# Routing the rows of a mixture of experts in five smaller batches instead of four, in one fused transformer kernel

## What is computed

```python
x = x + L0_xattn(layernorm(x), ctx, ctx)       # 16 heads, a temperature per head from a small network
x = x + L0_ffn(layernorm(x))
x = x + L1_xattn(layernorm(x), ctx, ctx)       # 8 heads, dilated windows
x = x + L1_ffn(layernorm(x))                   # 8 small experts
...
def L0_ffn(x, norm_scale, w_router, w_up, w_down):
    xn = rms_norm(x, norm_scale)
    scores_topk, idx = top_k(xn @ w_router.T, 2)          # 2 of 8 experts for each row
    weights = softmax(scores_topk)
    u, gate = split(moe_linear(each row twice, idx, w_up))  # row i times the weights of expert idx[i]
    down = moe_linear(u * silu(gate), idx, w_down)
    return sum(down * weights) + x
```

## Time and profile before

| | us |
|---|---|
| runs, median of 3 | 415.34 (414.65 to 415.39) |
| profiled execution, its own time | 413.28 |
| span of the profiled execution | 411.5 |
| busy in the span: PE | 353.8 |
| busy in the span: DVE | 303.3 |
| busy in the span: ACT | 271.8 |
| busy in the span: POOL | 196.9 |
| POOL, 32 scatters (line 942) | 32.2 |

### The profile page before, as it was taken

The page is one execution under the profiler, slowest core; times in us unless marked ns, Lnnn a source line. Parts: engine busy times, 40 slices in busy tenths (PEclk is TensorE's granted clock), DMA queues, the critical chain, the costliest instruction groups (busy, mean ns, idle before and its releaser), DMA issues.

```text
span 411.5 us, 11910 instructions
## 1 busy us (share of the span) xinstructions
PE 353.8 (86%) x4049; PEld 269.5 (65%) x4049; DVE 303.3 (74%) x1127; ACT 271.8 (66%) x813; POOL 196.9 (48%) x295
## 2 busy tenths in 40 slices
PE   2988897682599999973999999888999999968997
PEld 0524362341276767752999998757888888756886
DVE  5399989988428999996764444378898888885852
ACT  2499998986265657542578886457878778672440
POOL 4785878811002215667783000478878783532200
PEclk9988789986589999995799999989999999996999
DMA  7975739700000000112343332111001010000011
GB/s 234 338 212 160 223 100 335 322 1 0 3 2 6 6 5 18 37 34 70 105 116 92 97 92 57 37 33 41 27 23 28 17 28 2 2 2 2 4 49 51
DMA packets 36202, 30.97 MB, mean 75 GB/s; under 512 B 3504, under 2 KB 33584, under 8 KB 35504
## 3 DMA queue, kind: packets, MB, share of 16 engines
q1 hardware_dynamic: 33520, 24.98, 19.2%
q0 software_dynamic: 2048, 4.20, 3.5%
q10 hardware_dynamic: 576, 1.05, 0.7%
HBM read 14.94 MB, written 15.14 MB: 73 GB/s over the span
## 4 chain that ended last, share of the span: by engine, by line
PE 56%; DVE 19%; ACT 9%; issue 8%; POOL 4%; DMA 4%; POOLq 0%; DVEq 0%; SPq 0%; ACTq 0%
PE psum L1753 9%; ACT wa L649 6%; PE psum L1705 5%; PE psum L1545 4%; PE psum L1781 4%; PE psum L1764 4%; DVE scored L1089 3%; DVE scored L1076 3%; PE psum L1585 3%; PE psum L1894 3%; PE psum L1804 2%; PE psum L1688 2%; PE psum L1857 2%; DVE work L1131 2%; PE psum L1820 2%
## 5 line engine op out<-in xcount | busy, mean ns | idle before, releaser
L649 ACT ACTIVATE wa<-psum,scored 128x120 f32<-128x120 f32 x256 | 69.5, 436 | 3.8 <-DVE scored L1076 3.8
L983 POOL DMA_INDIRECT c_area<-by_expert,rows_at x32 | 31.4, 980 | 51.3 <-DMA by_expert<-c_area 39.7
L1089 DVE BATCH_NORM_STATS2 scored<-wa 128x6 f32<-128x240 f32 x128 | 43.1, 398 | 1.6 <-issue 0.8
L1076 DVE TENSOR_REDUCE scored<-psum 128x8 f32<-128x960 f32 x32 | 36.5, 1142 | 9.9 <-PE psum L1585 9.9
L682 ACT ACTIVATE work<-psum 120x1024 f32<-120x1024 f32 x32 | 31.0, 1021 | 18.8 <-PE psum L1693 18.8
L1753 PE MATMUL psum<-c_area,work 128*128 128x128 f32 x312 | 43.3, 284 | 0.0
L1585 PE MATMUL psum<-wa,qT 64*128 64x480 f32 x128 | 41.0, 725 | 2.3 <-ACT wa L649 2.3
L1753 PEld LDWEIGHTS psum<-c_area,work 128*128 128x128 f32 x312 | 39.7, 200 | 0.1
L910 POOL TENSOR_TENSOR rstd<-rstd,eps 128x2 f32<-128x2 f32 x16 | 12.5, 784 | 55.0 <-DVE rstd L1165 55.0
L866 POOL TENSOR_TENSOR wa<-kT,first 128x960 f32<-128x960 f32 x16 | 28.6, 1791 | 16.6 <-PE psum L1585 16.6
L942 POOL DMA_INDIRECT by_expert<-scored,rows_at x32 | 32.2, 1006 | 8.9 <-issue 8.3
(11 more groups left out here) (264 smaller groups left out, 945.0 us busy)
## 6 DMA issues: line engine op xcount, KB each, us to landing
by_expert<-work SPq DMA_DIRECT2D x12, 768.0 KB, 7.6
c_area<-by_expert SPq DMA_DIRECT2D x39, 64.0 KB, 1.8
by_expert<-c_area SPq DMA_DIRECT2D x39, 64.0 KB, 1.6
upT<-in_up_dram SPq DMA_DIRECT2D x1, 2048.0 KB, 13.7
work<-in_heads_dram SPq DMA_DIRECT2D x1, 1536.0 KB, 8.9
late<-in_late_dram SPq DMA_DIRECT2D x1, 1098.0 KB, 10.3
x<-in_x_dram ACTq DMA_DIRECT2D x4, 256.0 KB, 5.6
ctxS<-in_ctx_classes_dram SPq DMA_DIRECT2D x1, 1024.0 KB, 10.0
```

The lines of the kernel that those rows point to most:

```text
L649: e = nc.scalar.activation(prob[:, z, head, :], psum[:, score_bank(b, half) + h // 4, (h % 4) * LK:(h % 4 + 1) * LK], ACT.Exp, bias=rowneg ...
L983: nc.gpsimd.indirect_dma_start(y_rows[:, r, j, :], None, by_expert[:, :], bass.IndirectOffsetOnAxis(rows_at[:, i:i + 1], 0)).then_inc(ld_y ...
L1076: nc.vector.tensor_reduce(rowneg[:, b * H0:(b + 1) * H0].rearrange("p (a c h) -> p a c h", a=2, c=2)[:, :, half], banks(score_bank(b, half ...
L1089: s = nc.vector.bn_stats(bnout[:, bass.ds(b * HALF0 + h // 2, 1), :].rearrange("p a s -> p (a s)"), prob[:, z, h:h + 2, :].rearrange("p h ...
```

## The change

There are now five batches of 4, 3, 3, 3 and 3 sequences, so 8, 6, 6, 6 and 6 slots, and four phases of 7, 6, 6 and 20 tiles, after batches 1, 2, 3 and 4. The picks come in steps 9, 12, 15, 18 and 21 (before 9, 13, 17 and 21). The first table is two steps earlier. Scatters are two or three a step in steps 11 to 18, and the last twelve follow behind the steps. The pieces of the second table come in tiles 0 to 2, two a tile at first, those of the third in tiles 3 to 7 and of the fourth in tiles 8 to 12. In `pick_experts`, `place_rows` and `rank` the fixed numbers of sequences and slots give way to those of the batch. The core of the diff:

```diff
-BATCH = 4
-BATCHES, SLOTS = NB // BATCH, 2 * BATCH
+BATCH_SEQS = (4, 3, 3, 3, 3)
+BATCHES = len(BATCH_SEQS)
+BATCH_AT = tuple(sum(BATCH_SEQS[:r]) for r in range(BATCHES + 1))
+MOST_SLOTS = 2 * max(BATCH_SEQS)
...
+def slots_of(r):
+    return slice(2 * BATCH_AT[r], 2 * BATCH_AT[r + 1])
...
-        seqs = BATCH * (batch + 1)
+        seqs = BATCH_AT[batch + 1]
...
+def seq_at(i):
+    r = batch_of(i // 2)
+    return BATCH_AT[r] + (i - 2 * BATCH_AT[r]) % BATCH_SEQS[r]
...
-                            sp.wait_ge(scattered[r], 16 * SLOTS)
+                            sp.wait_ge(scattered[r], 16 * 2 * BATCH_SEQS[r])
...
-        PICK_AT = {BATCH * (r + 1) - 1 + LOGITS_B: r for r in range(BATCHES)}
-        TABLE_PIECES = 5
+        PICK_AT = {BATCH_AT[r + 1] - 1 + LOGITS_B: r for r in range(BATCHES)}
...
-        PIECES_AT = {15: ((0, 0),), 16: ((0, 1), (0, 2)), 17: ((0, 3),), 18: ((0, 4),)}
-        SCATTERS = {BATCH + LOGITS_B + 1 + i: range(2 * i, 2 * i + 2) for i in range((BATCHES - 1) * BATCH)}
+        PIECES_AT = {13: ((0, 0),), 14: ((0, 1), (0, 2)), 15: ((0, 3),), 16: ((0, 4),)}
+        SCATTERS_AT = ((11, 2), (12, 3), (13, 2), (14, 3), (15, 2), (16, 2), (17, 3), (18, 3))
+        SCATTERS, LOOPED = {}, 0
+        for step, count in SCATTERS_AT:
+            SCATTERS[step] = range(LOOPED, LOOPED + count)
+            LOOPED += count
+        TABLES_AT = {0: ((1, 0), (1, 1)), 1: ((1, 2), (1, 3)), 2: ((1, 4),), **{3 + i: ((2, i),) for i in range(5)},
+                     **{8 + i: ((3, i),) for i in range(5)}}
...
-                r = i // SLOTS
-                if i % SLOTS == 0:
+                r = batch_of(i // 2)
+                if i == 2 * BATCH_AT[r]:
                     pool.wait_ge(k_rows, r + 1)
                     pool.wait_ge(zeroed, 16 * (NB - 4))
...
-            for i in range(SLOTS * (BATCHES - 1), SLOTS * BATCHES):
+            for i in range(LOOPED, 2 * NB):
                 scatter(i)
...
-                if n in range(2 * TABLE_PIECES):
-                    tile_table(1 + n // TABLE_PIECES, n % TABLE_PIECES)
-                elif n == TILES - 4:
+                for piece in TABLES_AT.get(n, ()):
+                    tile_table(*piece)
+                if n == TILES - 4:
                     expert_weights()
```

More of the change, by code:

```diff
@@ L43, with batch_of, seqs_of @@
 GROUPS = NB // SEQS
-BATCH = 4
-BATCHES, SLOTS = NB // BATCH, 2 * BATCH
+BATCH_SEQS = (4, 3, 3, 3, 3)
+BATCHES = len(BATCH_SEQS)
+BATCH_AT = tuple(sum(BATCH_SEQS[:r]) for r in range(BATCHES + 1))
+MOST_SLOTS = 2 * max(BATCH_SEQS)
+def batch_of(b):
+    return next(r for r in range(BATCHES) if b < BATCH_AT[r + 1])
+def seqs_of(r):
+    return slice(BATCH_AT[r], BATCH_AT[r + 1])
+def slots_of(r):
+    return slice(2 * BATCH_AT[r], 2 * BATCH_AT[r + 1])
 class Phase:
     def __init__(self, batch, first_tile):
-        seqs = BATCH * (batch + 1)
+        seqs = BATCH_AT[batch + 1]
         self.batch, self.last, self.first_tile = batch, seqs == NB, first_tile
@@ L84, in slot_of @@
 def slot_of(j, b):
-    r, i = divmod(b, BATCH)
-    return SLOTS * r + BATCH * j + i
+    r = batch_of(b)
+    return 2 * BATCH_AT[r] + BATCH_SEQS[r] * j + b - BATCH_AT[r]
+def seq_at(i):
+    r = batch_of(i // 2)
+    return BATCH_AT[r] + (i - 2 * BATCH_AT[r]) % BATCH_SEQS[r]
 def residue(c):
@@ L165, in packs @@
                  ("expert_rows", expert_rows.reshape(P, -1))])
-    ranks = Pack([("tri", np.triu(np.ones((P, P)), 1)), ("region_rows", np.tile(np.arange(NE) * REGION, (P, SLOTS))),
+    ranks = Pack([("tri", np.triu(np.ones((P, P)), 1)), ("region_rows", np.tile(np.arange(NE) * REGION, (P, MOST_SLOTS))),
                   ("tile_no", np.tile(np.arange(MOST_TILES), (P, 1))),
@@ L338, in build @@
         tri_b, ones_b = halves(0), halves(1)
-        region_b = halves(2, SLOTS * NE)[0:1]
+        region_b = halves(2, MOST_SLOTS * NE)[0:1]
         seen = halves(3, BATCHES * NE).rearrange("p (r e) -> p r e", e=NE)
@@ L382, in build @@
         logits1 = keep[:, 256:384].rearrange("p (b e) -> p b e", b=NB)
-        rank_ps = keep[:, 512 - SLOTS * NE:512]
+        rank_ps = keep[:, 512 - MOST_SLOTS * NE:512]
         total_ps = keep[0:1, 192:192 + NE]
@@ L942, in scatter @@
                 nc.gpsimd.indirect_dma_start(by_expert[:, :], bass.IndirectOffsetOnAxis(rows_at[:, i:i + 1], 0),
-                                             xrow[:, BATCH * r + i % BATCH, :], None).then_inc(scattered[r], 16)
+                                             xrow[:, seq_at(i), :], None).then_inc(scattered[r], 16)
             def b_scatter(b, z):
@@ L1209, in pick_experts @@
             def pick_experts(r):
-                of, at = slice(BATCH * r, BATCH * (r + 1)), slice(SLOTS * r, SLOTS * (r + 1))
+                of, at, n = seqs_of(r), slots_of(r), BATCH_SEQS[r]
                 nc.vector.tensor_tensor(rt[:, 0, of], mx8[:, of, 1], mx8[:, of, 0], ALU.subtract).then_inc(k_diff, 1)
@@ L1215, in pick_experts @@
                 k_done(nc.vector.tensor_tensor(picked[:, at].rearrange("p (j b) e -> p j b e", j=2),
-                                               iota.unsqueeze(1).unsqueeze(1).to_broadcast([P, 2, BATCH, NE]),
-                                               rt[:, 4:6, of].unsqueeze(3).to_broadcast([P, 2, BATCH, NE]), ALU.is_equal))
+                                               iota.unsqueeze(1).unsqueeze(1).to_broadcast([P, 2, n, NE]),
+                                               rt[:, 4:6, of].unsqueeze(3).to_broadcast([P, 2, n, NE]), ALU.is_equal))
                 k_after()
@@ L1223, in place_rows @@
             def place_rows(r):
-                at = slice(SLOTS * r, SLOTS * (r + 1))
-                own = small[:, 0, 0:SLOTS * NE].rearrange("p (i e) -> p i e", e=NE)
+                at, n = slots_of(r), 2 * BATCH_SEQS[r]
+                own = small[:, 0, 0:n * NE].rearrange("p (i e) -> p i e", e=NE)
                 dve.wait_ge(k_rank, r + 1)
-                k_done(nc.vector.tensor_tensor(own, rank_ps.rearrange("p (i e) -> p i e", e=NE), picked[:, at], ALU.mult))
+                k_done(nc.vector.tensor_tensor(own, rank_ps[:, 0:n * NE].rearrange("p (i e) -> p i e", e=NE), picked[:, at], ALU.mult))
                 for k, p in enumerate(PHASES):
@@ L1231, in place_rows @@
                 k_after()
-                row = small[:, 0, SLOTS * NE:SLOTS * (NE + 1)]
+                row = small[:, 0, n * NE:n * (NE + 1)]
                 k_done(nc.vector.tensor_reduce(row, own, AX_X, ALU.add))
@@ L1721, in rank @@
                     pe.wait_ge(k_rows, r)
-                cells = rank_ps.rearrange("p (i e) -> p i e", e=NE)
+                cells = rank_ps[:, 0:n * NE].rearrange("p (i e) -> p i e", e=NE)
                 nc.tensor.matmul(cells, tri_b[:, :], picked[:, at], start=True, stop=False)
                 if r:
-                    nc.tensor.matmul(cells, ones_b[:, :], seen[:, r - 1, :].unsqueeze(1).to_broadcast([P, SLOTS, NE]),
+                    nc.tensor.matmul(cells, ones_b[:, :], seen[:, r - 1, :].unsqueeze(1).to_broadcast([P, n, NE]),
                                      start=False, stop=False)
-                for i in range(SLOTS - 1):
+                for i in range(n - 1):
                     nc.tensor.matmul(cells[:, i + 1:], ones_b[:, :],
-                                     picked[:, at.start + i, :].unsqueeze(1).to_broadcast([P, SLOTS - 1 - i, NE]), start=False, stop=False)
-                m = nc.tensor.matmul(rank_ps, ones_b[0:1, :], region_b, start=False, stop=True)
+                                     picked[:, at.start + i, :].unsqueeze(1).to_broadcast([P, n - 1 - i, NE]), start=False, stop=False)
+                m = nc.tensor.matmul(rank_ps[:, 0:n * NE], ones_b[0:1, :], region_b[:, 0:n * NE], start=False, stop=True)
                 if r in [p.batch for p in PHASES]:
```

## The result

The changed kernel takes 416.18 us in the median of 20 runs (412.15 to 418.26), the kernel before 414.99 us on the same chip (20 runs, 410.60 to 417.41). The ratio is **1.0048, 95% interval 1.0027 to 1.0070**: slower, by 1.1 to 2.9 us. The ratio is of the fast runs alone, so it is not the quotient of the two medians (1.0029). On the scale of the forecast that is 415.34 x 1.0048 = 417.3 us, above 415.6 us and just above the end of the range, 416.9 us. The profiled execution's own time is 417.37 us (before 413.28).

A forecast was written before the change was run, and what follows sets the result against it. The first phase was taken to wait for the sixteenth scatter, with DVE idle 3.35 us. The hand-over's -0.07 and the first tiles' +0.39 gave +0.3 us: 415.6 us on the runs' scale, range 413.4 to 416.9 us.

The forecast's parts named there:

- The gate: Ahead of tile 0: first phase needs 14 scatters, issued earlier; at most DVE's 3.35 us of waiting would go.
- DVE's surplus: Up to sequence 14's variance: an added pick, place and table pieces delay the root of 14 by 3.0 us, to 186.73.
- Rival 1: Faster: added routing delays DVE's steps by only 1.5 instead of 3.0 us, gain 1.2 us, 414.2 us; chance 0.16.
- POOL's third scatter: Between the roots of 14 and 15: three scatters instead of two, root of 15 at 191.39, DVE stands 1.9 us.
- rival 4: Slower: scatters behind a busy DVE last 1.55 instead of 0.96 us, three add 1.8 us, 417.4 us; chance 0.12.
- the prediction's tenths of a microsecond: Scatters beside a full DVE: DVE and POOL lengthen each other by tenths of a microsecond, no more.
- The clock: PE's granted clock at the first tiles: no gain counted, since PE's wait for the load becomes one for the norm.
- Rival 2: Faster: PE's clock stays up, first two tiles take 2.56 us less, gain 2.2 us, 413.1 us; chance 0.08.
- Among the first tiles: After tile 0: a second table piece on DVE costs 0.39 us; the additional piece 4 is taken as nothing.
- rival 3: Slower: piece 4 of the first late table costs its whole 1.01 us at tile 3, 416.7 us; chance 0.18.
- The rest costs nothing: Added rank matmuls run while PE waits; the 15 leftover scatters land before the load behind tile 12's store, margin over 1 us.

The follow-up runs named there:

- six versions with an earlier tile 0: Kernel before with scatters packed earlier; changed kernel with scatters 17 and 18 moved last, also with four-value loads; three versions with batches 4, 3, 4, 5: 0.9928 to 0.9990.
- Without the short loads: Changed kernel with tables padded to 8, 8, 8 and 20 tiles, so every register load takes four values: 415.92 us, 1.0018.
- late scatters: Changed kernel with the six scatters of steps 17 and 18 moved behind the root of sequence 15: 413.71 us, 0.9990.
- four batches: Changed kernel with batches of 4, 3, 4, 5 and scatters looped only in steps 11 to 16: 412.39 us, 0.9932; with four-value loads too: 412.92 us, 0.9954.
- both single repairs: Changed kernel with scatters looped only in steps 11 to 16 and register loads of four values: 412.91 us, 0.9971.

## Why the prediction was wrong

**The gate, right.** The wait for the sixteenth scatter went, and with it the 3.35 us.

**DVE's surplus, right.** Root of sequence 14: 189.09 - 2.40 = 186.69 on the scale of before; forecast 186.73. Rival 1 (routing not passed on whole) is out.

**POOL's third scatter, right.** Root of 15 at 193.57 - 2.40 = 191.17, forecast 191.39; DVE idle for it 1.63 us, forecast 1.9; eviction of tile 0 at 194.16, forecast 194.42. The scatters lasted 1.03 and 0.96 us beside a busy DVE and 0.95 while DVE idled for POOL: rival 4 is out. The rule of the Trainium skill, "SBUF — State Buffer" (section "A bandwidth-pool intuition that's wrong"), that such a DMA waits beside certain DVE copies, does not show here, as far as these operations go. The prediction read all 32 scatters as standing next to a full DVE. Some of them did not; in the 3.35 us in which DVE idled they lasted as long as the median:

```profile
192.20 0.96 POOL L942 DMA_INDIRECT by_expert<-scored,rows_at  x1 [0.30 <-issue]
```

So that DVE and POOL lengthen each other is not shown; the prediction's tenths of a microsecond are at most an upper bound.

**The clock, right not to count on it.** The granted clock after was 0.50 (1.2 GHz) from 189.4 us on, with PE busy for 0.94 us of the three from 187, and rose to 1.00 (2.4 GHz) only at 203.1, 5.8 us after tile 0's projection began; before, 5.4 us (200.66 - 195.23). Rival 2 names a real lever, though: the six versions with an earlier tile 0 had the clock back over 3 us sooner. Windows of the change (busy PE, PEld, DVE, ACT, POOL, granted clock, DMA):

```profile
190.00:193.00 3.00, 0.70 (x8) 0.42 (x8) 2.47 (x14) 0.37 (x1) 2.39 (x3) 0.50 0.39 117
...
199.00:202.00 3.00, 2.82 (x20) 2.53 (x20) 2.65 (x13) 0.89 (x2) 2.30 (x3) 0.50 0.27 81
202.00:205.00 3.00, 3.00 (x23) 2.96 (x23) 2.04 (x12) 1.82 (x5) 2.18 (x3) 0.82 0.21 67
```

**Among the first tiles, right in size for what was counted, in part by luck.** Without the short loads the stretch is 23.01 - 22.55 = +0.46 us, forecast +0.39. Only 0.25 of it stands where the forecast had it, from tile 0 to tile 1 (2.95 instead of 2.70 us). Piece 4 did cost something, at tiles 8 and 12 (0.49 and 0.35 us) and hardly at tile 3 (0.12), where rival 3 had it, and the steps that had waited for a piece 4 before (tile 4 to 5 and tile 8 to 9) paid for it by 0.51 and 0.32.

**"The rest costs nothing" is the step that failed.** A term was missing from the sum. Phases of 7, 6 and 6 tiles do not only move tables: their lengths set how many values each `read_four` takes, so the load at tile 4 takes three instead of four, and the one at tile 11 two. Three values take 0.78 to 0.86 us instead of 0.31 to 0.33, on ACT ahead of the weight copy and on PE ahead of the down projection. Without the short loads the first fourteen tiles took 1.00 us less, 0.62 of it at the load of three. That size belongs to this arrangement: with late scatters the same repair gave 0.26 us, with four batches 0.49, and the kernel before lost 0.3 for each load of three. The slowness was not in any row of the busy views, since a register load does not count as busy; the rows of the queues had it, and the trace of before already held loads of one, two and four values (0.32, 0.49 and 0.31 us on ACT), though none of three. One more reading under this head was wrong, at no cost: the load of tile 7 already needs three of the 15 scatters that are left over and that of tile 13 nine, not first that of tile 19 behind the store of tile 12. SP waited for scatters only once, for 2.0 us, ahead of tile 0.

The trace's sum from the mark is then: hand-over -0.36, first tiles +0.46, the short loads +1.00, and 0.5 behind the last tile, +1.6 us. What the 0.5 is stays open; no run tried it. By the forecast's own terms 0.3 + 1.0 = 1.3 us, 416.6 us, would have been in the range and in the interval of the runs. The range was too narrow for a sum whose every unlisted term stood at nothing.

## What to carry over

When a change alters a count that helpers divide by (here tiles of a phase, read four at a time), follow the count into the remainders: the odd last group can cost more than a full one. To open a gate early, first move the cheap work that holds it (two scatters into steps with room on POOL gave 0.9963, with no new table or pick), and look at what stands between the last two waits of the queue that it passes. Padding a group to its full size, with values that are never used, cost nothing that the trace shows here. When a kernel starts a stage earlier, read the granted clock too before the gain is put down to the gate.

## What was not expected of the hardware

**A register load of four values is as fast as one of a single value, and three take longest.** On ACT one value took 0.32 us and two 0.49 in the trace of before:

```profile
L476 ACTq TENSOR_LOAD <-tile_tab x1: 317/317/317, 208.7 to 208.7; - x1
...
L476 ACTq TENSOR_LOAD <-tile_tab x1: 488/488/488, 251.2 to 251.2; - x1
```

Three took 0.69 to 0.86, four 0.31 in the median; the first load of an execution is longer (four values 0.51, three 1.01). The Trainium skill, "Runtime: NRT & Kernel Launch" (section "Instruction fetch mechanics"), gives about 200 ns a register for register loads. The page describes them as loads from HBM, and this table lies on the chip. From one to three values the rows agree with steps of about 0.2 us, the four-value load does not, and the measurement decides.

**A clock that goes down at another moment moves the time with no change in the lists.** Of the 2.40 us ahead of the mark, some 1.6 arise between 83 and 88 us, in a part that the change does not touch. PE's timeline, the same 16 matmuls of before, of the change, and of the version with both single repairs, which has the same lists there as the change:

```profile
82.62 1.92 PE L1606 MATMUL psum<-small,work 128*128 128x1 f32 x16 [1.31 <-issue]
```
```profile
83.39 3.34 PE L1630 MATMUL psum<-small,work 128*128 128x1 f32 x16 [1.30 <-issue]
```
```profile
83.08 1.92 PE L1631 MATMUL psum<-small,work 128*128 128x1 f32 x16 [1.31 <-issue]
```

The granted clock fell to 0.50 at 83.6 us in the change, in the middle of them, and at 84.6 and 85.3 in the other two, behind them. The last one reaches the mark at 159.39 us, close to before's 158.92. Comparing spans without a common mark would have put these 2.4 us on the change.
